# Attention's picking comparison made by ScalarE in a graph network's edge loop, with GpSimd's rescaling and half of a product moved

## The reference, cut to what matters

```python
wk = mlp2(edge_features, k_w1, k_b1, k_w2, k_b2)
wv = mlp2(edge_features, v_w1, v_b1, v_w2, v_b2)
k = tensor_product(x_dst, edge_sh, wk, Cqk)       # sum over 9 sh of sh * (x_e @ C[:, s]), times w
v = tensor_product(x_dst, edge_sh, wv, Cv)
attn = einsum('ehd,ehd->eh', q[edge_src], k)
amax = segment_max(attn, edge_src)
ex = exp(attn - amax[edge_src])
denom = segment_sum(ex, edge_src)
upd = segment_sum(v * alpha, edge_src)            # alpha = ex / denom
```

## Time and profile before

| what | value |
|---|---|
| median of 3 runs | 5087.5 us (5077.75 to 5090.65) |
| the profiled execution | 5084.4 us, its span 5082.7 us |
| the attention loop | about 1065 to 3870 us of the span |
| TensorE, VectorE busy, whole span | 86%, 80% |
| ScalarE, GpSimd busy, whole span | 51%, 47% |

### The profile page before, as it was taken

How to read it: one execution, slowest core, us unless ns; L and a number is a source line. 1 busy time by engine, 2 the same in 40 slices (tenths; PEclk the granted TensorE clock), 3 DMA queues, 4 the chain that set the end, 5 groups by cost and what they waited for, 6 DMA issues and landing times. The chain is left out here.

```text
span 5082.7 us, 93633 instructions
## 1 busy us (share of the span) xinstructions
PE 4378.5 (86%) x21874; PEld 3160.3 (62%) x21874; DVE 4062.3 (80%) x9260; ACT 2575.0 (51%) x5924; POOL 2381.0 (47%) x2660
## 2 busy tenths in 40 slices
PE   1787877879999999999999999999998677777777
PEld 0222343457777777777777777777777566666665
DVE  5999965469999999999999999999994455555554
ACT  0777750047777777777777777777773100000000
POOL 1000000035555555555555555555552477777774
PEclk9999988879999999999999999999997555555555
DMA  2112115378888887888788888788882344444442
GB/s 57 76 76 98 79 51 232 145 165 180 180 180 180 178 180 179 181 179 181 178 179 182 180 180 181 177 181 180 179 181 52 76 100 103 101 103 103 102 103 63
DMA packets 576585, 719.35 MB, mean 142 GB/s; under 512 B 204519, under 2 KB 338727, under 8 KB 572583
## 3 DMA queue, kind: packets, MB, share of 16 engines
q1 hardware_dynamic: 517910, 634.65, 50.5%
q0 software_dynamic: 52288, 81.11, 8.1%
q10 hardware_dynamic: 6288, 2.48, 0.2%
HBM read 663.58 MB, written 54.36 MB: 141 GB/s over the span
## 5 line engine op out<-in xcount | busy, mean ns | idle before, releaser
L1341 POOL DMA_INDIRECT attn_rows<-x_twice,attn_idx x808 | 960.0, 1188 | 237.5 <-issue 203.9
L1696 POOL DMA_INDIRECT msg_rows<-a_rows,msg_idx x808 | 779.0, 964 | 370.2 <-issue 243.6
L1547 DVE TENSOR_TENSOR attn_z<-attn_xt,attn_sh 128x512 f32<-128x512 f32 x1010 | 681.8, 691 | 67.7 <-ACT attn_xt L1259 42.9
L1282 ACT CAST attn_z_hi<-attn_z 128x512 fp32r<-128x512 f32 x1010 | 606.8, 623 | 204.0 <-DVE attn_z L1547 197.6
L1360 POOL TENSOR_TENSOR acc_den<-acc_den,attn_sums 128x256 f32 x808 | 582.7, 721 | 188.7 <-POOL acc_den L1360 151.9
L1734 PE MATMUL msg_at_dst<-msg_bwin,msg_pick 128*128 128x64 f32 x1616 | 397.6, 428 | 271.1 <-DVE msg_pick L1760 218.7
L1734 PEld LDWEIGHTS msg_at_dst<-msg_bwin,msg_pick 128*128 128x128 f32 x1616 | 359.8, 328 | 351.3 <-DVE msg_pick L1760 263.1
L1674 ACT ACTIVATE msg_msg<-msg_pre 128x256 f32<-128x256 f32 x202 | 84.2, 417 | 941.8 <-DVE msg_pre L1775 937.7
L1553 DVE TENSOR_TENSOR attn_z_lo<-attn_z,attn_z_hi 128x512 fp32r<-128x512 f32 x808 | 555.0, 687 | 1.0 <-ACT attn_z_hi L1282 0.8
L1362 POOL MEMSET acc_den<- 128x6656 f32 x1 | 5.6, 5645 | 980.2 <-POOLq L90 980.2
L538 PE MATMUL count_bank<-count_key_hot,count_lo_hot 128*128 128x400 bf16 x1395 | 330.7, 348 | 135.9 <-DVE count_key_hot L496 132.1
(11 more groups left out here) (294 smaller groups left out, 10985.6 us busy)
## 6 DMA issues: line engine op xcount, KB each, us to landing
attn_sh<-in_edge_sh SPq DMA_DIRECT2D x404, 640.0 KB
attn_dst<-dst_scaled SPq DMA_DIRECT2D x202, 256.0 KB
attn_qwin<-q_rows SPq DMA_DIRECT2D x808, 64.0 KB
attn_mask<-dst_step SPq DMA_DIRECT2D x202, 256.0 KB, 3.5
msg_dst<-dst_scaled SPq DMA_DIRECT2D x202, 256.0 KB, 3.2
counts<-chunk SPq DMA_DIRECT2D x15, 3100.0 KB, 9.7
chunk_late<-counts SPq DMA_DIRECT2D x15, 3100.0 KB, 10.3
attn_feat<-in_edge_feat SPq DMA_DIRECT2D x404, 64.0 KB
```

What stands on the lines that cost most here:

```text
L1282: nc.scalar.copy(z_hi[p][:, c, :], z[:, c % 2, :]).then_inc(high_sb, 1)
L1341: pool.indirect_dma_start(rows[p][:, t, :], None, dram["x_twice"], bass.IndirectOffsetOnAxis(ap=idx[p][:, t:t + 1], axis=0)).then_inc(rows ...
L1547: dve.tensor_tensor(z[:, c % 2, :], xt[p][:], sh[p][:, c, :], ALU.mult).then_inc(z_ready, 1)
L1696: pool.indirect_dma_start(rows[p][:, t, :], None, dram["a_rows"], bass.IndirectOffsetOnAxis(ap=idx[p][:, t:t + 1], axis=0)).then_inc(rows_ ...
```

## The change

ScalarE makes the pick in the way it makes the onehot: four Abs of 128 x 128 (`pick_apart`) between wv and vt, and one Relu (`make_pick`) behind the onehot's. VectorE's comparison is gone. VectorE's fifth low half moves from ahead of u's first half to between the two halves. GpSimd's rescaling becomes a step of its own, `fade(g+1)`, placed behind `add(g)` and ahead of the gather; it waits for the exponentials of its group and for the backward scan of the group after it.

```diff
+            def pick_apart(g, n, p):
+                act.wait_ge(dst_in[p], 16 * (n + 1))
+                if not (is_first(g, 0) or is_first(g, 1)):
+                    act.wait_ge(q_ps, g - 1)
+                for t in range(TG):
+                    nc.scalar.activation(pick[p][:, t, :], dst[p][:, t * P:(t + 1) * P], ACT.Abs, scale=-1.0,
+                                         bias=sb["node_of_part"][:, bass.ds(TG * g + t, 1)]).then_inc(pick_apart_sb, 1)
+            def make_pick(g, p):
+                act.wait_ge(pick_apart_sb, TG * (g + 1))
+                nc.scalar.activation(pick[p][:], pick[p][:], ACT.Relu, scale=-1.0, bias=sb["ones"][:, 0:1]
+                                     ).then_inc(pick_ready, 1)
 # ScalarE, body
                 if front:
                     nc.scalar.activation(wv[:], b_wv_den[:], ACT.Identity, bias=sb["L2_v_b2"][:, 0:1]).then_inc(w_sb, 1)
+                if has_two(g):
+                    pick_apart(*in_two(g, n, p))
                 if back:
                     act.wait_ge(vt_ps, g)
...
                 if front:
                     make_onehot(g, p)
+                if has_two(g):
+                    make_pick(g + 2, p)
                 if has_two(g):
                     take_rows(*in_two(g, n, p))
 # ScalarE, first: pick_apart and make_pick behind take_rows, for groups 0 and 1
 # GpSimd
+            def fade(g, p):
+                base = nc.values_load_multi_w_load_instructions(
+                    sb["dst_i"][0:1, bass.ds(TG * g, 1)], engines=[mybir.EngineType.Pool], min_val=0, max_val=PADN,
+                    skip_runtime_bounds_check_because="dst holds node numbers below N, and PADN")[1][0]
                 factor = ex[p][:, GE:GE + 1].unsqueeze(1).to_broadcast([P, 2, 1])
-                pool.wait_ge(sum_sb, 2 * (g + 1))
-                pool.wait_ge(low_ready, KC * (min(g + 4, G) if isinstance(g, int) else g + 4))
+                pool.wait_ge(ex_sb, g + 1)
+                pool.wait_ge(topped, min(g + 2, G) if isinstance(g, int) else g + 2)
                 if not is_first(g, 0):
                     pool.wait_ge(added, STEPS * g)
                 pool.sem_inc(pool_go, 1)
-                first_col = sb["acc_den"][:, :, bass.ds(bases[0], 1)]
+                first_col = sb["acc_den"][:, :, bass.ds(base, 1)]
                 pool.tensor_tensor(first_col, first_col, factor, ALU.mult).then_inc(added, 1)
+            def add(g, p):
+                bases = window_bases(nc, mybir.EngineType.Pool, sb, TG * g)
+                pool.wait_ge(sum_sb, 2 * (g + 1))
+                pool.wait_ge(low_ready, KC * (min(g + 4, G) if isinstance(g, int) else g + 4))
                 for t in range(TG):
                     pool.wait_ge(added, STEPS * g + t + 1)
...
             with pool.Fori(0, G // 2 - 3) as n:
                 add(2 * n + 1, 1)
+                fade(2 * n + 2, 0)
                 gather(2 * n + 6, n + 3, 0, False)
                 add(2 * n + 2, 0)
+                fade(2 * n + 3, 1)
                 gather(2 * n + 7, n + 3, 1, False)
 # VectorE
-            def make_pick(g, n, p):
-                dve.wait_ge(dst_in[p], 16 * (n + 1))
-                if not (is_first(g, 0) or is_first(g, 1)):
-                    dve.wait_ge(q_ps, g - 1)
-                dve.tensor_tensor(pick[p][:], dst[p][:].rearrange("p (t e) -> p t e", t=TG),
-                                  sb["node_of_part"][:, bass.ds(TG * g, TG)].unsqueeze(2).to_broadcast([P, TG, P]),
-                                  ALU.is_equal).then_inc(pick_ready, 1)
...
                 low(*group, KC - 2)
-                low(*group, KC - 1)
...
                     dve.tensor_tensor(u[:], b_k[:], wk[:], ALU.mult).then_inc(kw_ready, 1)
+                if next:
+                    low(*after(g, n, p), KC - 1)
+                if front:
                     dve.wait_ge(q_ps, g + 1)
                     dve.wait_ge(kw_ready, g + 1)
                     dve.tensor_tensor(u[:], b_q[:], u[:], ALU.mult).then_inc(u_ready, 1)
...
-                if has_two(g):
-                    make_pick(*in_two(g, n, p))
                 if front:
                     maxima(g, n, p)
```

More of the change, by code:

```diff
@@ L1167, in attention_loop @@
                                 "kw_ready", "u_ready", "vw_ready", "dve_set"))
-        xt_sb, hid_sb, w_sb, ex_sb, vt_sb, sum_sb, high_sb, apart = (
-            ph.sem(n) for n in ("xt_sb", "hid_sb", "w_sb", "ex_sb", "vt_sb", "sum_sb", "high_sb", "apart"))
+        xt_sb, hid_sb, w_sb, ex_sb, vt_sb, sum_sb, high_sb, apart, pick_apart_sb = (
+            ph.sem(n) for n in ("xt_sb", "hid_sb", "w_sb", "ex_sb", "vt_sb", "sum_sb", "high_sb", "apart",
+                                "pick_apart"))
         vx_ready = ph.sem("vx_ready")
@@ L1321, in first @@
                 take_rows(g, n, p)
+                pick_apart(g, n, p)
+                make_pick(g, p)
                 for c in range(3):
@@ L1327, in first @@
                 take_rows(*after(g, n, p))
+                pick_apart(*after(g, n, p))
+                make_pick(g + 1, 1 - p)
             stage_idx(0, 0)
@@ L1343, in gather @@
                         bass.IndirectOffsetOnAxis(ap=idx[p][:, t:t + 1], axis=0)).then_inc(rows_in[p], 16)
-            def add(g, p):
-                bases = window_bases(nc, mybir.EngineType.Pool, sb, TG * g)
+            def fade(g, p):
+                base = nc.values_load_multi_w_load_instructions(
+                    sb["dst_i"][0:1, bass.ds(TG * g, 1)], engines=[mybir.EngineType.Pool], min_val=0, max_val=PADN,
+                    skip_runtime_bounds_check_because="dst holds node numbers below N, and PADN")[1][0]
                 factor = ex[p][:, GE:GE + 1].unsqueeze(1).to_broadcast([P, 2, 1])
-                pool.wait_ge(sum_sb, 2 * (g + 1))
-                pool.wait_ge(low_ready, KC * (min(g + 4, G) if isinstance(g, int) else g + 4))
+                pool.wait_ge(ex_sb, g + 1)
+                pool.wait_ge(topped, min(g + 2, G) if isinstance(g, int) else g + 2)
                 if not is_first(g, 0):
@@ L1369, in _ @@
             gather(4, 2, 0, False)
+            fade(0, 0)
             add(0, 0)
+            fade(1, 1)
             gather(5, 2, 1, False)
@@ L1373, in _ @@
                 add(2 * n + 1, 1)
+                fade(2 * n + 2, 0)
                 gather(2 * n + 6, n + 3, 0, False)
                 add(2 * n + 2, 0)
+                fade(2 * n + 3, 1)
                 gather(2 * n + 7, n + 3, 1, False)
-            add(G - 5, 1)
-            for g in range(G - 4, G):
+            for g in range(G - 5, G - 1):
                 add(g, g % 2)
+                fade(g + 1, (g + 1) % 2)
+            add(G - 1, 1)
         @block.sync
@@ L1618, in first @@
             def first(g, n, p):
-                make_pick(g, n, p)
                 split_begin(g, n, p)
                 split_end(g, n, p)
-                make_pick(*after(g, n, p))
+                low(g, n, p, KC - 1)
             dve.wait_ge(dve_set, 4)
```

## The result

The changed kernel took 5121.4 us (median of 5 runs, 5108.35 to 5127.44) against 5089.67 for the kernel before (5 runs, 5077.75 to 5090.65): a ratio of 1.0064, 95% interval 1.0054 to 1.0075. It is slower by 0.64%; 5027 was forecast. The profiled execution took 5127.44 us, its span 5125.8.

The account below looks back on a forecast made before the run. The loop from z over VectorE's chain to u, then TensorE and xt, was taken to set the 13.86 us period. 198 x 0.31 = 61 us saved, 2 added, gave 5025, 5027 as a median; range 5008 to 5064.

Parts of the forecast that it names:

- Rescaling as a step of its own.: GpSimd: the gather starts about 1 us later, paid for by 3.55 us of idle time a group; cost 0, range 0 to 0.3.
- rival 2: VectorE's products are slowed by gathers behind the backward scan; 0.32 us a group, 5086 us; chance 0.08 together with another rival.
- the loop through u, TensorE and xt sets the period: A group runs from z over VectorE's chain to u (8.13 us), then TensorE and xt back to z (5.74 us).
- the new order: VectorE's fifth low half between u's halves saves 0.25 to 0.37 us a group, taken as 0.31; u's second half at 7.82.
- the removed pick: Taking the pick off VectorE brings the scans 0.15 us earlier and buys slack, 0.52 us, but by itself moves no z.
- the forward and the backward scan: VectorE's forward scan would start 9.73 us and its backward scan 11.05 us behind z.
- ScalarE's cover: The pick's 2.0 us a group on ScalarE fit its idle 1.38 us before vt and 1.61 us before xt; cost 0.
- rival 3: dst lands too late for ScalarE's pick; at worst 1.2 us a group more than before, 5322 us; chance 0.04.
- Rival 1: GpSimd's addition holds VectorE's backward scan for its whole length, 0.73 us, overrunning the slack by 0.21; 5066 us; chance 0.08.
- the case "slower": The changed kernel is slower than before; chance 0.06: dst landing late 0.04, the rest partial losses on ScalarE or GpSimd.

Follow-up runs that it names:

- e3: The changed kernel with sh's transfers cut to one row of five from the third group on; 0.9933 of the kernel before.
- e12: The changed kernel with GpSimd's order of before (rescaling heads the additions, gather behind them) and sh cut to one row of five; 0.9905 of the kernel before.
- e2c: The kernel before with only the rescaling split off as a step ahead of the gather, on the first kind of chip; 1.0039 of the kernel before.
- e11c: The changed kernel without the rescaling step (rescaling heads the additions, gather behind them), on the first kind of chip; 0.9961 of the kernel before.
- e7: The kernel before with only the pick moved to ScalarE; 1.001 of the kernel before.
- e10: The changed kernel with the gather a group earlier, ahead of the additions, and the rescaling back at their head; 0.9878 of the kernel before, 0.9910 in a repeat.
- e4: The changed kernel with the gather a group earlier, ahead of the additions and the rescaling step; 0.9904 of the kernel before.
- e8: The kernel before with only the gather moved ahead of the additions, a group earlier; 0.9983 of the kernel before.
- e1: The changed kernel with the gather moved ahead of the rescaling step, still behind the additions; 1.0062 of the kernel before, then 1.0040 and 1.0063.

## Why the prediction was wrong

**The step that failed** is "*Rescaling as a step of its own.* ... the gather starts about 1 us later against its group. GpSimd's 3.55 us of idle time pay for it, and the rows are used a whole group later. Cost 0 (range 0 to 0.3, rival 2)". Late rows cost 0.40 us a group: 0.26 came by the step (14.01 - 13.70, less 0.05 for the held scan) and 0.13 by the shorter period, for which the prediction had no term. Three parts of it failed.
1. By medians over the loop the first issue of a gather moved from 11.77 to 13.87 us behind z, 2.1 and not 1: the wait for the backward scan and its wait for the fourth addition add up, and 0.6 us follow the rescaling in which nothing is shown. The last issue moved from 2.43 to 3.80 of the next body, past both sh transfers (1.8 and 2.6 in before).
2. Idle time of the issuing engine pays for the issue, not for the landing. The rows are used 14.6 us after the first issue in the kernel before, which is the whole group, but only 10 us after the last. I never looked for the transposes that read these rows, nor for the DMA share in the stretch between; that share was 1.06 in two of the 2 us stretches of before's group too.
3. The latency was taken as that of a quiet moment. By medians the last packet ends 2.3 to 2.6 us after the last issue without sh (e3, e12), 7.6 in the changed kernel and 8.3 in before. From the last issue to the transposes before had 10.05 us, and 1.78 of them were left when the last packet had ended. The step alone leaves 8.80 (e2c), the shorter period alone 9.11 (e11c), both together 8.55, and at the last packet 1.12, 1.06 and 0.92: in all three TensorE begins to wait, most in the last.

The place against sh counts more than the microseconds do. Sorted by how many of a gather's four issues stand ahead of sh's second transfer, the 189 groups of before's loop fall into 75 with all four, where the last packet ends 5.9 us after the last issue and 4.2 us are left, and 113 with three, where it ends 8.2 us after and 1.5 are left. In e7 all four are ahead in 153 groups, hence its 4.08 in the table at the same 10.05. In the changed kernel two are ahead in 152 groups, and the matmuls waited over 0.15 us in 85 of those, but only in 1 of the 30 with three ahead.

The Trainium skill (DMA: Bandwidth & Descriptors, "Issuing engines are not separate DMA queues") says that transfers started by different engines run on the same 16 DMA engines and interleave. The trace agrees: GpSimd's gather and SyncE's sh are on different queues, and the one took three times as long beside the other (7.6 against 2.3 to 2.6 us). That rule spoke against this step, and the prediction didn't weigh it.

**The size.** With 13.56 forecast and 13.57 measured in e10, the lost time is 14.01 - 13.61 (changed against e4) = 0.40 us a group, 79 us, for rows, near the 73 us that TensorE's weight loads stood idle for them, and 10 us for the held scan. Of the 102 us between forecast and profiled time some 13 are left; the loop itself grew by only about 31 of the 43 us between the two profiled spans, so they seem to lie outside it, and their cause is open.

**Right:** the loop through u, TensorE and xt sets the period; the new order shortens the way to u, in the groups shown by 0.30 us (7.83 against 8.13), by medians over the loop by 0.25 (7.84 against 8.09), where 0.31 was taken; the removed pick is slack only (e7); the forward and the backward scan to 0.01 us; ScalarE's cover; dst, for which no pick waited, so rival 3 is out. That the period of e10 hit the forecast to 0.01 us is in part luck: at the old order the early gather alone brings it from 13.86 to 13.82 (e8), and from there the order saves 0.25. Rival 2 is out too: products stayed at 0.69 and the first pair at 1.29. Rival 1, that an addition holds the scan for its whole length, is out: in the group shown first the scan should have ended at 2638.83, ended at 2639.35, and thus went on at 2638.13, 0.14 us before the end of the addition (2637.54 + 0.73). It is 0.14 to 0.15 in all 158 scans of the loop that were held. But cost 0 for it was too low, 0.05 us a group; by the prediction's own figures a long addition that starts right ahead of the scan holds it 0.73 - 0.14 = 0.59 us, more than the slack of 0.52. **None of the rivals** was the one that came; the case "slower" had been bound to dst, but for 0.02.

## What to carry to other kernels

When a DMA's issue moves, find its user and write down three numbers: issue, landing under the traffic that is then in flight, use. Idle time on the issuing engine says nothing on the last two. And where one large transfer fills the DMA engines for half of each period, a small and urgent one belongs ahead of it, or a whole period earlier: here, on the second kind of chip, moving the gather turned 1.0081 into 0.9904, and without the extra step into 0.9878. And before idle times are added up, see whether two of them are the same wait.

## What the runs showed of the hardware

- Who comes first, holds: in e11c the fourth addition started 0.03 us behind the backward scan, and it was the addition that lasted 1.63 us instead of 0.73, while the scan took its 1.22. In the changed kernel it is the other way round (1.74 and 0.73).
- On chips of the second kind TensorE's signals for the hidden layer and for wk came up to 2.6 us behind the shown ends of their matmuls, in kernels in which a late gather meets sh's transfers, and hardly at all when sh was cut (e3) or the gather was a group earlier (e4, e10): at most 3 such updates in any of these traces. SyncE showed register moves of more than 0.5 us on these chips in every kernel (35 to 92 between 1200 and 3700 us, none on the first kind). What is slow there, the runs don't show. So e1 is judged on such chips alone, and what it does on the first kind stays open.
- GpSimd's four issues of a gather stand 1.25 us apart where each takes 0.95. Beside VectorE's work they take up to 1.7 and stand up to 2.0 apart, as the first two do in the kernel before (median 2.01). In every 28th group, 7 of the changed kernel's loop, 2.21 us pass behind the first, with nothing shown that GpSimd waits for. TensorE's matmuls waited for the rows in 2 of these 7 and in 88 of 189 groups in all, so it isn't what makes the rows late; what causes it is open.
